# A two-layer decoder on one core: the three layer norms and the mask row of the first phase go from VectorE to ScalarE, and that phase's steps are put in a new order

## The reference, cut to what matters

```python
x = x + mamba(layernorm(x))                        # ln1: in-projection, conv of 4 taps, 32-head scan, gate, rms norm, out-projection
x = x + cross_attention(layernorm(x), ctx, mask0)  # ln2: 16 heads; scores get -10000 * (1 - mask0)
x = x + shared_ffn_and_routed_experts(layernorm(x))# ln3: top 2 of 16 experts
x = x + causal_attention(layernorm(x))
x = x + latent_attention(ctx, layernorm(x), mask1)
x = x + ternary_linear(layernorm(x))

def layernorm(x):  # no weights
    return (x - mean(x)) / sqrt(var(x) + 1e-5)
```

## Time and profile before

| what | value |
|---|---|
| median of three executions | 5043.33 us (5036.94 to 5046.49) |
| the profiled execution, its own time | 5044.57 us |
| its span | 5042.9 us |
| busy in the span: PE, DVE, ACT, POOL | 4273.5, 3676.8, 2829.3, 2671.5 us |
| mean granted clock of PE | 0.91 |
| the first phase | from the start to about 2760 us |

### The profile page before, as it was taken

One profiled execution on the slowest core, in us unless ns is written; L12 is line 12 of the kernel. 1 busy time (PEld: TensorE's weight loads), 2 busy tenths in 40 slices (PEclk: granted clock), 3 DMA queues, 4 the chain that ended last, 5 costly groups with the idle time before them and its releaser, 6 DMA issues.

```text
span 5042.9 us, 118113 instructions
## 1 busy us (share of the span) xinstructions
PE 4273.5 (85%) x33430; PEld 3115.1 (62%) x33431; DVE 3676.8 (73%) x8924; ACT 2829.3 (56%) x6774; POOL 2671.5 (53%) x3708
## 2 busy tenths in 40 slices
PE   3877777887777877778776988999999999999998
PEld 2655556665556655556554775666666666666665
DVE  3777777777777777777774545777777777777776
ACT  2555555555555555555553444666666666666564
POOL 3555555555555555555552234555555555555554
PEclk8889888888888888888887998999999999999999
DMA  5222222222222222222222440111111111111110
GB/s 149 71 71 73 73 74 75 78 71 71 71 71 71 71 71 71 72 72 72 71 71 77 145 129 28 30 30 30 31 32 31 33 30 30 30 30 33 29 31 22
DMA packets 215885, 304.09 MB, mean 60 GB/s; under 512 B 56608, under 2 KB 167456, under 8 KB 215840
## 3 DMA queue, kind: packets, MB, share of 16 engines
q1 hardware_dynamic: 188864, 240.33, 15.3%
q0 software_dynamic: 19200, 52.45, 3.2%
q10 hardware_dynamic: 7776, 10.75, 0.7%
HBM read 239.19 MB, written 64.23 MB: 60 GB/s over the span
## 4 chain that ended last, share of the span: by engine, by line
PE 46%; POOL 20%; issue 16%; DVE 7%; DMA 6%; SPq 3%; POOLq 1%; ACT 0%; DVEq 0%; ACTq 0%
PE Q L1374 13%; POOL arena L609 9%; PE Q L1379 8%; DMA arena<-cum_rows 6%; PE Q L1367 6%; PE Q L1396 3%; PE Q L1712 3%; PE Q L1745 3%; PE Q L1566 3%; PE Q L1402 2%; DVE arena L806 2%; POOL mvX L576 2%; PE Q L1411 2%; PE Q L1578 1%; POOL arena L597 1%
## 5 line engine op out<-in xcount | busy, mean ns | idle before, releaser
L1379 PE MATMUL Q<-ident,arena 128*128 128x128 f32 x4768 | 807.9, 290 | 305.2 <-DVE arena L749 262.6
L1379 PEld LDWEIGHTS Q<-ident,arena 128*128 128x128 f32 x4768 | 555.2, 145 | 566.4 <-DVE arena L749 282.0
L609 POOL TENSOR_TENSOR arena<-arena 128x1024 f32<-128x1024 f32 x256 | 497.8, 1961 | 121.2 <-DMA arena<-cum_rows 120.9
L1374 PE MATMUL Q<-Wkvl,arena 128*128 128x512 f32 x1024 | 499.6, 600 | 0.0
L756 DVE TENSOR_REDUCE mx<-Q 128x4 f32<-128x512 f32 x512 | 344.3, 683 | 175.1 <-PE Q L1396 170.5
L673 POOL TENSOR_TENSOR l<-l,half_pow 128x8 f32<-128x8 f32 x192 | 318.5, 1659 | 231.0 <-DVE l L1017 229.1
L698 POOL TENSOR_TENSOR arena<-arena,part_of 128x512 f32<-128x512 f32 x256 | 263.8, 1042 | 196.6 <-DVE part_of L1055 196.6
L1129 ACT ACTIVATE arena<-Q 128x256 f32<-128x256 f32 x256 | 98.3, 384 | 441.1 <-PE Q L1379 441.1
L1396 PE MATMUL Q<-arena 32*128 32x128 f32 x4096 | 302.2, 290 | 0.0
L806 DVE SCALAR_TENSOR_TENSOR arena<-arena,convw 128x128 f32<-128x128 f32 x768 | 298.1, 449 | 2.4
L1402 PE MATMUL Q<-ident,arena 128*128 128x128 f32 x2048 | 296.9, 279 | 1.8 <-ACT arena L1143 0.8
(11 more groups left out here) (303 smaller groups left out, 10851.8 us busy)
## 6 DMA issues: line engine op xcount, KB each, us to landing
arena<-cum_rows SPq DMA_DIRECT2D x256, 512.0 KB, 6.4
arena<-routed_rows SPq DMA_DIRECT2D x144, 128.0 KB, 2.1
expert_rows<-arena POOLq DMA_DIRECT2D x144, 128.0 KB, 2.0
arena<-in_x_dram SPq DMA_DIRECT2D x128, 128.0 KB, 6.2
arena<-in_ctx_dram SPq DMA_DIRECT2D x128, 128.0 KB, 2.1
x_rows<-arena SPq DMA_DIRECT2D x128, 128.0 KB, 1.7
arena<-x_rows SPq DMA_DIRECT2D x128, 128.0 KB, 2.3
out_dram<-arena SPq DMA_DIRECT2D x64, 128.0 KB, 1.7
```

The lines of the kernel that those rows point to most:

```text
L609: tell(g.tensor_tensor(E8[j], E8[j], cums[:, 8 * j:8 * j + 8].unsqueeze(2).broadcast_to([P, 8, T]), ALU.subtract), "diff")
L1374: last = mm(out, lhs(c), rhs(c), start=c == 0, stop=c == n - 1)
L1379: last = nc.tensor.transpose(out[:, c * P:(c + 1) * P], src[:, c * P:(c + 1) * P], ident[:, :])
```

## The change

It does four things, all in phase 1.

1. DVE no longer applies the norms: `moments` takes mean and variance only. POOL's `centre` makes two columns in four one-column instructions instead of two: -mean, var + eps, its power -0.5, and the product -mean * rstd. ACT's `normal` applies them in one activation (Identity, with scale = rstd and bias = -mean * rstd, both pointers to a column for each partition).
2. The mask row is made by ACT, for 128 values instead of 512; PE's mask matmul reads them four times through a broadcast view.
3. The guards that protected the old writes move along with them (for ln3, the wait for the scattered rows of the sequence before now stands on ACT).
4. ORDER's table for phase 1 is new on all five engines.

```diff
-            Yc Xm Ncb0 Ncb1 Ncb2 Ncb3 Mx Fm Nx Fo Mco
+            Ncb0 Ncb1 Ncb2 Yc Xm Mx Ncb3 Nx Mco Fm Fo
         "POOL": """
-            Nd0 Nd1 Mln1 Fln3 Xx1r Xln2 Nd2 Nd3 Msp Fsc Nm3 Nyg Nrms
+            Nd0 Nd1 Nd2 Xx1r Fln3 Xln2 Mln1 Nd3 Msp Nm3 Fsc Nyg Nrms
         "DVE": """
-            Mln1 Fln3 Xln2 Mln1n Fln3n Nm0 Xln2n Yk Xmr Fr Nm1 Mdt Ftop Msp Fslot Xm0 Xm1 Nm2 Fhg Vcv Xm2 Xm3 Vcv1 Fxo Vcv2 Vcv3 Ny0 Vxs2 Vcb Ny1 Vxdt Xho Vgz Nx1
+            Fln3 Xln2 Nm0 Mln1 Fr Yk Ftop Mdt Fslot Msp Xm0 Xm1 Fhg Nm1 Nm2 Xm2 Xm3 Fxo Vcv Vcv1 Vcv2 Vcv3 Ny0 Vxs2 Ny1 Vcb Vxdt Vgz Nx1 Xho
         "ACT": """
-            Ng0 YcT Ne0 Ng1 Mln1n Fln3n Ne1 Vbc Xln2n Frx Mab Xq Yv Ng2 Ne2 Ng3 Ne3 Vxp Fth NYt0 Mcum Xm0 Xm1 FhT Xm2 Xm3 NYt1 Xt0 Xt1 Vcth Xt2 Xt3 Nsq XOT NyT
-            Vtz
+            Ng0 YcT Ne0 Ng1 Fln3 Xln2 Fln3n Xmr Xln2n Mln1 Frx Mln1n Xq Mab Vbc Ne1 Ng2 Yv Fth Ne2 Ng3 FhT Ne3 Xm0 Xm1 Vxp Xm2 Mcum Xm3 NYt0 Xt0 NYt1 Xt1 Vcth Xt2
+            Xt3 Nsq XOT NyT Vtz
         "PE": """
-            YcT Yk Yv Mln1n Fln3n Vbc Fr Xln2n Mdt Xq Vip1 Vip1h Frk Xs0 Fgu Fguh Nv0 Nv1 Mcum Xs2 FhT Nv2 Fdn Nv3 Xt0 Ny0 Xt1 VCB Xt2 Ny1 Xt3 Xpv Xpv0 VxsT Xpv1
-            Xpv2 Xpv3 NyT Vz XOT Vzh Npr Nprh
+            YcT Yk Nv0 Fln3n Yv Xln2n Fr Mln1n Xq Vbc Mdt Frk Xs0 Fgu Fguh Vip1 Vip1h FhT Xs2 Fdn Mcum Nv1 Nv2 Xt0 Nv3 Xt1 Ny0 Xt2 VCB Ny1 Xt3 Xpv Xpv0 VxsT Xpv1
+            Xpv2 NyT Xpv3 Vz Vzh Npr Nprh XOT
...
-        mrow = sb("mrow", [P, NG, T], F16)
+        mrow = sb("mrow", [P, T], F16)
...
+            def centre(n, mv, b, c):
+
+                done(pool, f"{n}_var", b)
+                link(pool, c, b, g.tensor_tensor(mv[:, 4:5], mv[:, 0:1], eps[:, 2:3], ALU.mult))
+                link(pool, c, b, g.tensor_tensor(mv[:, 2:3], mv[:, 1:2], eps[:, 0:1], ALU.add))
+                link(pool, c, b, g.tensor_tensor(mv[:, 3:4], mv[:, 2:3], half_pow[:, 0:1], ALU.pow))
+                tell(g.tensor_tensor(mv[:, 5:6], mv[:, 4:5], mv[:, 3:4], ALU.mult), f"{n}_rstd")
...
+            def moments(n, src, st, mv, c, b):
+                link(dve, c, b, v.bn_stats(st[:, :], src), bare=True)
+                tell(v.bn_aggr(mv[:, 0:2], st[:, :]), f"{n}_var")
...
-                yield from norm("ln2", x1, xn2, stX, mvX, "X_DVE", b, "ln2n")
-                yield "mr"
-                done(dve, "mask0_in", b, 16)
-                tell(v.scalar_tensor_tensor(mrow[:, :, :], mask0i[:, :].unsqueeze(1).broadcast_to([P, NG, T]), 1.0,
-                                            ones[:, :].unsqueeze(1).broadcast_to([P, NG, T]), ALU.mult, ALU.subtract), "mrow")
+                moments("ln2", x1, stX, mvX, "X_DVE", b)
...
+            def normal(n, src, dst, mv, b):
+                done(act, f"{n}_rstd", b)
+                tell(s_.activation(dst, src, ACT.Identity, bias=mv[:, 5:6], scale=mv[:, 3:4]), f"{n}_xn")
...
+                yield "ln2"
+                normal("ln2", x1, xn2, mvX, b)
+                yield "mr"
+                done(act, "mask0_in", b, 16)
+                was(act, "S0", b, 4)
+                tell(s_.activation(mrow[:, :], mask0i[:, :], ACT.Identity, bias=eps[:, 2:3]), "mrow")
...
+                yield "ln3"
+                was(act, "scattered", b, 32)
+                normal("ln3", x2, xnF, mvF, b)
...
-                        mm(banks[j][:, :], mask_w[r, :], mrow[r, :, :], start=True, stop=False)
+                        mm(banks[j][:, :].rearrange("p (g k) -> p g k", g=NG), mask_w[r, :], mrow[r, :].unsqueeze(1).broadcast_to([32, NG, T]), start=True, stop=False)
```

More of the change, by code:

```diff
@@ L183, in two_layers @@
         half_pow = sb("half_pow", [P, XH])
-        eps = sb("eps", [P, 2])
+        eps = sb("eps", [P, 3])
         base = sb("base", [P, NE])
@@ L248, in two_layers @@
         stM, stX, stF, stA, stC, stK, stT = (sb(f"st{c}", [P, 6]) for c in "MXFACKT")
-        mvM, mvX, mvF, mvA, mvC, mvK, mvT = (sb(f"mv{c}", [P, 4]) for c in "MXFACKT")
+        mvM, mvX, mvF, mvA, mvC, mvK, mvT = (sb(f"mv{c}", [P, 6]) for c in "MXFACKT")
         ss0 = sb("ss0", [P, 4])
@@ L274, in two_layers @@
         sig("gathered", 32)
-        signals("M", "DVE", "ln1_var ln1_xn dt_pre ratio")
+        signals("M", "DVE", "ln1_var dt_pre ratio")
         signals("M", "PE", "ln1_Tps dt cumps")
-        signals("M", "ACT", "ln1_T dt_abs dt_exp cums cumT")
+        signals("M", "ACT", "ln1_xn ln1_T dt_abs dt_exp cums cumT")
         signals("M", "POOL", "ln1_rstd a")
@@ L287, in two_layers @@
         signals("Y", "ACT", "ctxT v0c")
-        signals("X", "DVE", "ln2_var ln2_xn mrow S0max:4 x2")
+        signals("X", "DVE", "ln2_var S0max:4 x2")
         signals("X", "PE", "ln2_Tps q0 S0:4 PT0ps:4 PV0:2")
-        signals("X", "ACT", "ln2_T q0c P0:4 PT0s:4 OT0")
+        signals("X", "ACT", "ln2_xn mrow ln2_T q0c P0:4 PT0s:4 OT0")
         signals("X", "POOL", "x1r ln2_rstd")
-        signals("F", "DVE", "ln3_var ln3_xn rmax sel slot hh xo")
+        signals("F", "DVE", "ln3_var rmax sel slot hh xo")
         signals("F", "PE", "ln3_Tps rout rank gu hTps down")
-        signals("F", "ACT", "ln3_T rexp gth hT")
+        signals("F", "ACT", "ln3_xn ln3_T rexp gth hT")
         signals("F", "POOL", "ln3_rstd")
@@ L320, in two_layers @@
         signals("T", "POOL", "lno_rstd ln7_rstd")
-        links = {"M_DVE": 3, "V_DVE": 3, "X_DVE": 5, "F_DVE": 15, "A_DVE": 5, "C_DVE": 1, "K_DVE": 2, "T_DVE": 7, "M_POOL": 11, "N_POOL": 1, "X_POOL": 1,
-                 "F_POOL": 1, "A_POOL": 1, "C_POOL": 2, "K_POOL": 4, "T_POOL": 2}
+        links = {"M_DVE": 3, "V_DVE": 3, "X_DVE": 5, "F_DVE": 15, "A_DVE": 5, "C_DVE": 1, "K_DVE": 2, "T_DVE": 7, "M_POOL": 13, "N_POOL": 1, "X_POOL": 3,
+                 "F_POOL": 3, "A_POOL": 1, "C_POOL": 2, "K_POOL": 4, "T_POOL": 2}
         steps = {}
@@ L541, in _ @@
             g.memset(eps[:, 1:2], 16.0 * RMS_EPS)
+            g.memset(eps[:, 2:3], -1.0)
             g.memset(onesb[:], 1.0)
@@ L576, in rstd @@
                 tell(g.tensor_tensor(mv[:, 3:4], mv[:, 2:3], half_pow[:, 0:1], ALU.pow), f"{n}_rstd")
+            def centre(n, mv, b, c):
[4 more added lines that the diff above has]
+                tell(g.tensor_tensor(mv[:, 5:6], mv[:, 4:5], mv[:, 3:4], ALU.mult), f"{n}_rstd")
             def M(b):
                 yield "ln1"
-                rstd("ln1", mvM, b, "M_POOL")
+                centre("ln1", mvM, b, "M_POOL")
                 yield "sp"
@@ L627, in X @@
                 yield "ln2"
-                rstd("ln2", mvX, b, "X_POOL")
+                centre("ln2", mvX, b, "X_POOL")
             def F(b):
                 yield "ln3"
-                rstd("ln3", mvF, b, "F_POOL")
+                centre("ln3", mvF, b, "F_POOL")
                 yield "sc"
@@ L781, in M @@
                 done(dve, "xa_in", b, 16)
-                yield from norm("ln1", xa, xn0, stM, mvM, "M_DVE", b, "ln1n")
+                moments("ln1", xa, stM, mvM, "M_DVE", b)
                 yield "dt"
@@ L876, in F @@
                 done(dve, "x2", b)
-                was(dve, "scattered", b, 32)
-                yield from norm("ln3", x2, xnF, stF, mvF, "F_DVE", b, "ln3n")
+                moments("ln3", x2, stF, mvF, "F_DVE", b)
                 yield "r"
@@ L1152, in M @@
             def M(b):
+                yield "ln1"
+                normal("ln1", xa, xn0, mvM, b)
                 yield "ln1n"
```

## The result

The changed kernel takes 4828.11 us (median of 4, 4826.19 to 4831.49) against 5042.57 us for the kernel before in the same runs: a ratio of 0.9573, with a 95% interval of 0.9560 to 0.9587. The forecast was 4883 us in a range of 4765 to 5040 us. The profiled execution's span is 4826.3 us.

A forecast was written before the change was run, and what follows sets the result against it. A loop of waits DVE, POOL, PE, DVE, mostly DVE, was taken to bound the body. Parts summed to 36.9 to 40.0 us, taken as 38.7: 2.6 us less over 62 bodies, 161 us off 5044.6, giving 4883; range 4765 to 5040.

The forecast's parts named there:

- the forecast's own case: Whole kernel: body of 36.9 to 40.0 us, 4771 to 4964 us, or 4989 with 0.4 us of unseen waits.
- The first part: Body from the x2 addition to PE's cumulative sum `Mcum`: 24.75 us before, 19.5 to 22.6 us after.
- the slow case: From x2 to `Mcum`, PE's clock falls again after its wait for `Nm0`: 22.6 us instead of 19.5.
- turn-taking with `Nm0`: Behind the variances, POOL's norm instructions take turns with DVE's `Nm0`, as both use SBUF: 1.2 us added.
- the four small steps: Router product, its maximum, its exponential and rank, before `Mcum`: about half a microsecond each, 2.1 us.
- The second part: Body from `Mcum` to the next x2: 16.55 us before, 17.4 us after, a growth of 0.85 us.
- a held `Xho`: Head output: POOL's `Nd0` to `Nd2` run without a break into `Xho`, holding its addition; 0.7 us, up to 1.7.
- the 2.15 us wait: DVE's wait for PE's scores before the third maximum goes, as they are asked for before `Mcum`.
- what the change removes: Four DVE instructions per body, norms and mask row: 5.59 of 30.7 us, in a loop said to be mostly DVE.
- The signs: If right: DVE busy about 25 us per body, norm activations 0.56, no third-maximum wait, period 38.7, ln3 power stretched.
- latency using up the gain: Norms pass DVE, POOL, ACT, PE, ACT; late `Nd2` delays them: body 40.4 to 41.4 us, 4989 to 5050; chance 0.12.
- half clock in the tail: `Vz`, `Npr` and `XOT` before x2 double at the lower clock: 3.9 us more, body 43.9, 5206 us; chance 0.10.

The follow-up runs named there:

- The filled kernel: Changed kernel plus 12 matmuls per body with unread results, cut to fit TensorE's waits (6, 3 and 3): 4747.54 us, ratio 0.9405.
- m3_on_dve: Changed kernel with the fourth block's product moved from GpSimd to VectorE, behind the last maximum: 4830.22 us, ratio 0.9573.
- order_alone: Kernel before with the changed kernel's order, norms and mask row staying on VectorE: 4826.06 us, ratio 0.9565.
- sp_order_back: Changed kernel with SyncE's order of before for loads and the cumulative sum's output: 4827.61 us, ratio 0.9567.
- mask_back: Changed kernel with the mask row back on VectorE, 512 wide: 4827.09 us, ratio 0.9568.
- pe_filled2: Changed kernel plus 15 matmuls per body with unread results, ten before `Nv0` and five before the cumulative sum: 4834.38 us, ratio 0.9613.

## Why the prediction was right, and which of its steps was not

**The time.** 4883 us was forecast, 4828 came; it lies inside the forecast's own case of 4771 to 4989. The body is 37.53 us, where I took 38.7 between 36.9 and 40.0. A saving of 3.78 us per body over 216 us is 57 full bodies; I had counted 62.

**The first part** was put at 19.5 to 22.6 us and is 21.03. Some terms held: ScalarE's norm 0.60 (0.56), mask row 0.39 (0.39), GpSimd's four instructions 1.35 without turn-taking (1.35; the ln2 norm, 1010.80 to 1012.15). The slow clock came as in the slow case, which was put at 22.6, so 1.6 us are left over. Three terms were too large: turn-taking with `Nm0` 0.5 us, not 1.2; `Yv` and the norm of x1 in front of the copy about 0.6, not 1.1; and the slow clock, which by this count costs the path some 1.6 us, not 3.1 (0.5 in the four small steps, 2.59 us instead of 2.1, and 1.1 in VectorE's steps up to the softplus, 5.76 instead of 4.67). One was too small: from GpSimd's softplus to `Mcum` it takes 7.64 us, not 6.9, as two of its instructions take 1.20 and 1.01 us beside `Nm1` and `Nm2`. The filled kernel agrees on the clock: its body is 1.32 us shorter.

**The second part** was put at 17.4 us and is 16.50. The 0.7 us for a held `Xho` did not come (0.426 us); the convolution beside `Nm3` cost 2.1 us in its first row, near what the old one had. The later `XOT` and `Xho` cost more than the 2.3 us that I took: from the end of the convolution to that of x2 it is 10.07 us (1035.39 to 1045.46), 7.23 before. Letting go the 2.15 us wait gave more: inside the new order, undoing that step alone costs 3.4 us per body (40.95 against 37.53).

**The step that failed** is the reading under "what the change removes", that the loop is mostly VectorE and the 5.59 us of norms and mask lie on it. With the new order those steps stay on VectorE at no cost (4826.06 against 4828.11 us), and without it their removal makes the kernel 0.45% slower. A row without idle time does not show that the work in it holds the body. The time came from the order: the variances right behind x2, and TensorE's `Xs2` and `Fdn` ahead of `Mcum`. The forecast came out all the same because the 5.59 us never enter its sum. The sum follows the path from x2 to `Mcum` and back in the new order; only the reason given for the gain was wrong. That its total is within some 1% is in part luck, as the terms above that were too large and too small offset each other.

**The signs.** Nearly all those named for "right" appeared: VectorE's busy time 26.1 us per body (about 25), the norms' activations 0.60 us, no wait before the third maximum, 37.53 us between the variances. In GpSimd's chain for ln3 the product is stretched, not the power. None of these signs could have told relief from order.

**The rivals.** The second, latency using up the gain, happened to the norms' move, and was hidden by the order's gain: GpSimd, ScalarE and TensorE in series behind x2 took what VectorE gave. The cause that I had named for it, a late `Nd2`, did not come: GpSimd was done with it at 1007.41 us and waited 0.70 us for x2. The third, half clock in the tail, did not come in the changed kernel: the clock is 1.00 there. The Trainium skill, "TensorE: Matmul & The Clock Gate", section What's actually happening, says that the throttled clock is the default and that activity releases it. The first part agrees: the clock falls to 0.50 behind a wait of 2.63 us, and with the waits filled the steady stage has 0.98 instead of 0.87. I had argued from the earlier trace rows that TensorE has slack. No filled kernel tests this for the kernel before; of the changed one it was wrong. The loads were costed at nothing, and that held.

## What to carry to other kernels

Undo each part alone before giving it the credit: here the change named first was worth nothing by itself and the re-ordering all of it. In a hand-ordered queue look first for a step that waits for a long chain of another engine and has ready work behind it; inside the new order, one such step in the wrong place costs 214 us of 5040. A step whose undoing costs the whole gain need not have given the whole gain: look at the parts of the body too. Price a relief of an engine together with the clock of TensorE: a shorter path that makes TensorE wait longer can be paid back at 1.2 GHz.

## What the runs showed that I had not expected

Six kernels with different work have the same mean body to 0.03 us: 37.53 (changed, m3_on_dve), 37.55 (order_alone, sp_order_back, mask_back, and pe_filled2, with 301.3 to 2366.7 us for 56 variances). It looks as if body and clock settle on each other, but the single bodies speak against one common length. In m3_on_dve the mean is made of bodies of 36.55 us (clock 0.95) and of 38.67 us (0.82), in pe_filled2 of 36.78 us (1.00) and 38.24 us (0.96); in the one of the latter that I read in single microseconds, the slow stretch stands at the attention values. What decides which bodies lose their clock was not measured, and whether the equal means are more than chance stays open. What is shown is that a small gain can be paid back in some of the bodies: in m3_on_dve all of it was.

Open too is whether moving `Xs2` and `Fdn` alone, in the kernel before, would give any of the gain; only the reverse was tried. The new orders of GpSimd and ScalarE were not undone alone either.

Useless matmuls made the kernel faster: 12 per body took 81 us off the changed kernel, 4747.54 against 4828.11.
